# A gated graph kernel: the adjacency product cut into 64x64x64 pieces, and w4's product reordered

## What the reference computes

```python
h = relu(layernorm(x))                       # first layer: attention
q, k, v = h @ Wq.T, h @ Wk.T, h @ Wv.T
rel = adj.T * (q @ k.T); rel = rel / norm(rel, axis=2)
x = x + rel @ v
h = relu(layernorm(x)); h0 = h               # second layer: a gated network, three steps
for _ in range(3):
    a = adj @ h                              # per graph; in and out matrix are the same adj
    z = sigmoid(w3([a, a]) + b3 + u3(h) + bu3)
    r = sigmoid(w4([a, a]) + b4 + u3(h) + bu3)
    hv = tanh(w5([a, a]) + b5 + u5(r * h) + bu5)
    h = (1 - z) * h + z * hv
x = x + h
```

## Time and profile before

| what | us |
|---|---|
| median of three runs | 908.33 |
| the profiled execution, its own time | 907.36 |
| its span on the core | 905.6 |
| PE busy | 891.7 |
| DVE (VectorE) busy | 756.7 |
| ACT (ScalarE) busy | 520.9 |
| POOL busy | 111.0 |

### The profile page before, as it was taken

One profiled execution on the slowest core, in us unless ns is written; L12 is line 12 of the kernel. 1 busy time (PEld: TensorE's weight loads), 2 busy tenths in 40 slices (PEclk: granted clock), 3 DMA queues, 4 the chain that ended last, 5 costly groups with the idle time before them and its releaser, 6 DMA issues.

```text
span 905.6 us, 15070 instructions
## 1 busy us (share of the span) xinstructions
PE 891.7 (98%) x4984; PEld 763.0 (84%) x4984; DVE 756.7 (84%) x1527; ACT 520.9 (58%) x892; POOL 111.0 (12%) x161
## 2 busy tenths in 40 slices
PE   8999999999999999999999999999999999999996
PEld 7878888888888888888888888888888888888885
DVE  6888879888799888988988888988879888798665
ACT  5465664656456564665645656556664656555552
POOL 2110102101021010210101101120101101020000
PEclk9999999999999999999999999999999999999998
DMA  6023222623235142441414513154221622233212
GB/s 182 6 69 114 93 94 99 203 69 113 90 123 184 46 142 89 140 167 42 150 58 141 184 69 116 46 176 148 93 93 70 203 98 93 93 116 117 87 54 93
DMA packets 75394, 98.73 MB, mean 109 GB/s; under 512 B 8176, under 2 KB 65776, under 8 KB 75376
## 3 DMA queue, kind: packets, MB, share of 16 engines
q1 hardware_dynamic: 75376, 98.50, 33.0%
HBM read 50.76 MB, written 47.71 MB: 109 GB/s over the span
## 4 chain that ended last, share of the span: by engine, by line
PE 95%; DVE 2%; issue 1%; DMA 1%; ACT 1%; SPq 0%; DVEq 0%
PE gate L410 14%; PE gate L411 14%; PE gate L412 14%; PE cand L410 10%; PE cand L412 9%; PE cand L411 9%; PE fea L564 9%; PE tok L410 3%; PE tok L411 2%; PE tok L412 2%; PE fea L497 2%; PE fea L411 1%; PE fea L410 1%; PE fea L412 1%; DMA x_s<-x 1%
## 5 line engine op out<-in xcount | busy, mean ns | idle before, releaser
L808 ACT ACTIVATE r_s<-gate,b_r 128x512 f32<-128x512 f32 x96 | 65.7, 690 | 123.8 <-PE gate L412 123.8
L1129 DVE TENSOR_TENSOR rh<-r_s,h 128x512 f32<-128x512 f32 x96 | 69.8, 760 | 29.5 <-ACT r_s L808 28.9
L821 ACT ACTIVATE z_s<-gate,b_z 128x512 f32<-128x512 f32 x96 | 64.1, 683 | 48.0 <-PE gate L412 48.0
L827 ACT ACTIVATE c_s<-cand,b_c 128x512 f32<-128x512 f32 x96 | 64.4, 686 | 26.2 <-PE cand L412 25.5
L724 ACT ACTIVATE h_hi<-h 128x512 fp32r<-128x512 f32 x92 | 56.8, 628 | 38.1 <-DVE h L921 22.4
L355 POOL TENSOR_TENSOR rstd<-vare,minus_half 128x4 f32<-128x4 f32 x32 | 42.0, 1312 | 297.3 <-DVE vare L955 297.3
L410 PE MATMUL gate<-h_hi,W_hi_u 128*128 128x512 f32 x192 | 77.9, 406 | 0.2 <-DVE h_lo L921 0.2
L1101 DVE SCALAR_TENSOR_TENSOR d_s<-z_s,h 128x512 f32<-128x512 f32 x96 | 63.5, 685 | 17.5 <-ACT z_s L821 17.5
L410 PE MATMUL cand<-rh_hi,W_hi_u 128*128 128x512 f32 x192 | 76.5, 398 | 0.0
L410 PE MATMUL gate<-a_hi,W_hi_w 128*128 128x512 f32 x192 | 75.0, 390 | 1.1 <-DVE a_lo L921 1.1
L411 PE MATMUL gate<-h_lo,W_hi_u 128*128 128x512 f32 x192 | 75.1, 391 | 0.0
(11 more groups left out here) (150 smaller groups left out, 2202.7 us busy)
## 6 DMA issues: line engine op xcount, KB each, us to landing
h_back<-h_trip SPq DMA_DIRECT2D x216, 128.0 KB, 2.8
h_trip<-h_turned SPq DMA_DIRECT2D x40, 512.0 KB, 2.6
out<-o_s SPq DMA_DIRECT2D x16, 512.0 KB, 3.8
x_s<-x SPq DMA_DIRECT2D x15, 512.0 KB, 4.9
hx_trip<-hx SPq DMA_DIRECT2D x14, 512.0 KB, 3.5
hx_back<-hx_trip SPq DMA_DIRECT2D x56, 128.0 KB, 2.8
h_trip<-h_blk SPq DMA_DIRECT2D x14, 512.0 KB, 3.0
h_trip_last<-h_turned SPq DMA_DIRECT2D x7, 512.0 KB, 3.5
```

The costliest lines, as they stand in the source:

```text
L808: nc.scalar.activation(r_s[:, c, :], gate[:, c, :], ACT.Sigmoid, bias=b_r[:, c:c + 1]).then_inc(r_ready, 1)
L821: nc.scalar.activation(z_s[:, c, :], gate[:, c, :], ACT.Sigmoid, bias=b_z[:, c:c + 1]).then_inc(z_ready, 1)
L827: nc.scalar.activation(c_s[:, c, :], cand[:, c, :], ACT.Tanh, bias=b_c[:, c:c + 1]).then_inc(c_ready, 1)
L1129: nc.vector.tensor_tensor(rh[:, c, :], r_s[:, c, :], h[s][:, c, :], ALU.mult).then_inc(rh_ready, 1)
```

## The change

Three parts. First, the adjacency product is 32 matmuls of 64x64 by 64x64 in place of eight of 128x128 by 128x128. Each takes 64 nodes (one graph, e) and 64 features (f) as stationary operand and one diagonal block of `adjT` as moving one. Graph e reads partitions of half e and writes into PSUM bank e; feature half f lands in output partitions of half f. So `fea` is now one bank for each graph of a pair, both chunks in it, and the two `split_a` work by bank e, writing a_hi and a_lo in runs of 64 columns. Both banks are released together at the end. A semaphore `sources_seen`, which nobody waits for, is incremented once or twice in each adjacency by TensorE's sequencer, behind the waits. Second, w4's product does all eight matmuls that take a_hi, then waits for a_lo, then does the four that take a_lo; the first output half (o = 0) now ends two matmuls before the second. Third, u3's and w4's product of window 1 move from the head of the loop to its foot, so that TensorE jumps back behind w4's product.

```diff
+        def set_columns(t, e):
+            return t[:].rearrange("p c (q e n) -> p c q e n", q=Q, e=2)[:, :, :, e, :]
+
+        def set_bank(e):
+            return fea[:, e, :].rearrange("p (c q n) -> p c q n", c=C, q=Q)
...
-            def adjacency(c, src, n):
-
-                fea_wait(n, c)
-                for q in range(Q):
-                    last = nc.tensor.matmul(fea[:, c, graph_pair(q)], src[:, q, c * P:(c + 1) * P], adjT[:],
-                                            start=True, stop=True)
-                last.then_inc(fea_full, 1)
+            def adjacency(src, n, t_full=None):
+                fea_wait(n, 1)
+                for c in range(C):
+                    if t_full is not None:
+                        pe.wait_ge(t_ready, t_full + c)
+                    if c == 0 or t_full is not None:
+                        pe.sem_inc(sources_seen, 1)
+                    for q in range(Q):
+                        for f in range(2):
+                            part = slice(c * P + f * N, c * P + (f + 1) * N)
+                            for e in range(2):
+                                last = nc.tensor.matmul(set_bank(e)[half(f), c, q, :], src[half(e), q, part],
+                                                        adjT[half(e), half(e)], start=True, stop=True)
+                last.then_inc(fea_full, 2)
...
             def reset_gate_a(w, s, n_a):
-                for c in range(C):
-                    pe.wait_ge(a_hi_ready, 2 * w + (c + 1))
-                    pe.wait_ge(fea_taken, 2 * n_a + (c + 1))
-                    for o in range(C):
-                        last = product(gate[:, o, :], weight("w4", c, o), (a_hi[s][:, c, :], a_lo[s][:, c, :]),
-                                       False, c == C - 1)
-                        if c == C - 1:
-                            last.then_inc(r_full, 1)
+                pe.wait_ge(a_hi_ready, 2 * w + 2)
+                for o in range(C):
+                    for c in range(C):
+                        w_hi, w_lo = weight("w4", c, o)
+                        one(gate[:, o, :], w_hi, a_hi[s][:, c, :])
+                        one(gate[:, o, :], w_lo, a_hi[s][:, c, :])
+                pe.wait_ge(fea_taken, 2 * n_a + 2)
+                for o in range(C):
+                    for c in range(C):
+                        last = one(gate[:, o, :], weight("w4", c, o)[0], a_lo[s][:, c, :], stop=c == C - 1)
+                    last.then_inc(r_full, 1)
...
+            def first_reset_gate(i):
+                pe.wait_ge(h_lo_new, 4 * i + 4)
+                reset_gate_h(6 * i + 1, 1)
+                reset_gate_a(6 * i + 1, 1, use_in_round("adj 0", i - 1))
...
+            first_reset_gate(0)
             with pe.Fori(0, PAIRS - 1) as i:
                 for k in (1, 2, 3, 4, 5):
                     window(i, k, lambda name: use_in_round(name, i))
                 window(i + 1, 0, lambda name: use_in_round(name, i))
+                first_reset_gate(i + 1)
...
-            def split_a(s, c, n):
-                fea_wait(n, c)
-                copy(a_hi[s][:, c, :], fea[:, c, :]).then_inc(a_hi_ready, 1)
+            def split_a(s, e, n):
+                fea_wait(n, e)
+                copy(set_columns(a_hi[s], e), set_bank(e)).then_inc(a_hi_ready, 1)
...
-                sub(a_lo[s][:, c, :], fea[:, c, :], a_hi[s][:, c, :]).then_inc(fea_taken, 1)
+                sub(set_columns(a_lo[s], e), set_bank(e), set_columns(a_hi[s], e)).then_inc(fea_taken, 1)
```

More of the change, by code:

```diff
@@ L186, in gated_graph_kernel @@
         tok_taken = sem("tok_taken")
+        sources_seen = sem("sources_seen")
         h_is_turned, h_out, h_in, t_ready = sem("h_is_turned"), sem("h_out"), sem("h_in"), sem("t_ready")
@@ L412, in product, with one @@
                 return nc.tensor.matmul(dst, l_lo, r_hi, start=False, stop=stop, skip_group_check=True)
+            def one(dst, lhs, rhs, start=False, stop=False):
+                return nc.tensor.matmul(dst, lhs, rhs, start=start, stop=stop, skip_group_check=True)
             def weight(n, c, o):
@@ L637, in window @@
                     pe.wait_ge(h_lo_new, 4 * i + 2)
-                elif k == 1:
-                    pe.wait_ge(h_lo_new, 4 * i + 4)
-                else:
+                elif k > 1:
                     pe.wait_ge(h_lo_ready, 8 * i + 2 * (k - 1))
-                reset_gate_h(w, s)
-                reset_gate_a(w, s, use("adj %d" % (k - 1)) if k > 1 else use_in_round("adj 0" if k else "adj 5", i - 1))
+                if k != 1:
+                    reset_gate_h(w, s)
+                    reset_gate_a(w, s, use("adj %d" % (k - 1)) if k else use_in_round("adj 5", i - 1))
                 candidate_a(w, s)
@@ L657, in window @@
                         pe.wait_ge(h0_plain, 2 * i + 1)
-                        adjacency(0, h0[o], use("adj 5"))
-                        adjacency(1, h0[o], use("adj 5"))
+                        adjacency(h0[o], use("adj 5"))
                 elif k == 0:
                     pe.wait_ge(h0_plain, 2 * i)
-                    adjacency(0, h0[o], use("adj 0"))
-                    adjacency(1, h0[o], use("adj 0"))
-                else:
-                    for c in range(C):
-                        pe.wait_ge(t_ready, 8 * i + 2 * k + (c - 1))
-                        adjacency(c, t_s, use("adj %d" % k))
+                    adjacency(h0[o], use("adj 0"))
+                else:
+                    adjacency(t_s, use("adj %d" % k), 8 * i + 2 * k - 1)
             pe.wait_ge(const_ready, 1)
@@ L696, in _ @@
             pe.wait_ge(adj_in, 32)
-            adjacency(0, h0[0], n("adj first"))
-            adjacency(1, h0[0], n("adj first"))
+            adjacency(h0[0], n("adj first"))
             reset_gate_h_start()
@@ L708, in _ @@
             candidate_rh(0, 0)
-            adjacency(0, h0[1], n("adj 0"))
-            adjacency(1, h0[1], n("adj 0"))
+            adjacency(h0[1], n("adj 0"))
             tok_done(n("new 0"))
+            first_reset_gate(0)
             with pe.Fori(0, PAIRS - 1) as i:
@@ L1053, in split_state, with split_a @@
                     sub(h_lo[o][:, c, :], h[o][:, c, :], h_hi[o][:, c, :]).then_inc(h_lo_ready, 1)
-            def split_a(v, s, c):
-                dve.wait_ge(a_hi_ready, 2 * v + (c + 1))
-                sub(a_lo[s][:, c, :], fea[:, c, :], a_hi[s][:, c, :]).then_inc(fea_taken, 1)
+            def split_a(v, s, e):
+                dve.wait_ge(a_hi_ready, 2 * v + (e + 1))
+                sub(set_columns(a_lo[s], e), set_bank(e), set_columns(a_hi[s], e)).then_inc(fea_taken, 1)
             def turn_h0(g, s, w):
```

## The result

After the change the kernel takes 918.42 us, the median of four runs (915.40 to 919.44), against 908.33 before: a ratio of 1.010 [1.0085, 1.0115]. It is 1% slower. The forecast was 887 us with a range of 882 to 906, so it was wrong in sign and outside its range.

The account below looks back on a forecast made before the run. TensorE (PE) was taken as the bound, busy 891.7 of 905.6 us. 907.36 - 23.5 (adjacency) + 0.6 + 1.4 (a_lo waits) - 0.3 (first window 1) = 885.6; with 0.97 for the median 886.5, said as 887; range 882 to 906.

Parts of the forecast that it names:

- Part three: the jump: TensorE's loop end: the 208 ns jump stays hidden behind w4's product; gain 0, keeping up to 1.4 us from being lost.
- The cover: At the jump behind w4's product: that product's 2.7 us hides the jump instruction of 208 ns.
- Part one: Adjacency product on TensorE: 1.28 us in place of 1.78, 0.50 saved each, 23.5 us over 47 adjacencies.
- Four in flight: 16 steps: New adjacency's 64 records overlap in fours: 16 steps of 0.056 us, 0.89 plus 0.39 for edges, 1.28 us.
- the rival at 927: Two records in flight: the adjacency costs 2.18 us, 0.40 more than before, 47 times 18.8 us, so 927; chance 0.14.
- the scores' 1.08 / 32: In the two-in-flight rival: PE's possible feeding limit from the scores' 32 records, given as 29 ns; 64 x 0.034 are 2.16.
- Part two: w4's product reordered: a_lo wanted 5.84 us behind the adjacency instead of 4.02, second a_lo ready at 5.55, 0.29 in time.
- 0.3 us in this window: w4's product without the reorder: PE arrives 4.02 us behind the adjacency and waits 0.3 us for a_lo.
- The waits for a_lo: PE waiting for VectorE's second a_lo: 0.6 us over seven rounds in window 1, 1.4 us in windows 5 and 0.
- the prediction's sign: In the profile after, a wait of PE for a_lo of 1 to 3 us in all would show the forecast right.
- Writing in runs of 64 columns: ScalarE's a_hi and VectorE's a_lo keep their size and only write in runs of 64 columns: costed at nothing.
- own range of 882 to 893: Whole kernel: range of the main forecast, with edges 0.1 us smaller or the waits doubled; chance 0.68.

Follow-up runs that it names:

- experiment with q innermost: The changed kernel with TensorE's rounds written out and q as innermost loop, so eight records in a row use one quarter of the array: 953.11 us, one run.
- written-out version: The changed kernel with TensorE's seven rounds written out instead of looped, so its sequencer never jumps: 893.59 us, ratio 0.9827 to the kernel before.
- VectorE's other order: The changed kernel with rounds written out, and both a_lo splits ahead of VectorE's second turn of the state: 888.74 us, ratio 0.9781 to before.

## Why the prediction was wrong

**The step that failed** is the whole of "Part three: the jump", and in it the sentence "Its instruction takes 208 ns and is hidden today ... behind w4's product, 2.7 us, it is. Gain 0". It took the price of the jump from a row of a 1315-instruction body and kept it for one of 1893. The prediction itself counts the records, 16 and then 64 for each adjacency; six windows of 48 more are 576 more instructions, and nothing asked what they cost beyond their matmuls. No rival named it either, and the range, made from what matmuls and VectorE might do, left it out. Measured: 4.1 us for the instruction, 4.1 us of the kernel per taken jump on average (3.1 to 5.6 by the traces, more where the clock falls), 24.8 in all. The section of the Trainium skill cited above names this danger, and it wasn't weighed.

The cover was wrong as well. "2.7 us" is the length of w4's product, but not what is queued when the sequencer gets to the jump. A wait on a semaphore holds the sequencer, and the one for a_lo stands in the middle of that product: VectorE's second a_lo ends at 504.51, the first matmul that takes it starts at 504.56, and the jump at 504.67. PE's timeline at the jump:

```profile
504.18 0.39 PE L422 MATMUL gate<-a_hi,W_lo_w 128*128 128x512 f32 x1
504.56 1.19 PE L422 MATMUL gate<-a_lo,W_hi_w 128*128 128x512 f32 x4
508.88 0.49 PE L417 MATMUL cand<-a_hi,W_hi_w 128*128 128x512 f32 x1 [3.12 <-issue]
```

Four matmuls lie behind the wait, 0.9 us at 0.228. Even so the move is worth 4.8 us here, and parts two and three together 0.26% with the old adjacency.

**Part one: right.** The chain has the adjacency and its first follower at

```profile
498.72 1.09 PE fea L581 x64
499.81 0.43 PE gate L417
```

1.09 + 0.43 - 0.23 = 1.29 against the 1.28 forecast; by whole windows without a late a_lo, 15.40 less 14.92 and 14.95, or 16.85 less 16.33 in windows 3 and 5, the saving is 0.45 to 0.52, some 22.6 us in all and not 23.5. "Four in flight: 16 steps" holds. The timeline cut just behind an adjacency's first record (294.800) and uncut:

```profile
294.77 0.29 PE L581 MATMUL fea<-adjT,t_s 64*64 64x64 f32 x4
```

```profile
294.77 1.16 PE L581 MATMUL fea<-adjT,t_s 64*64 64x64 f32 x64
```

Four records start within 0.03 us, though the program has the two records of each matmul together. The strict order of the Trainium skill, "TensorE: Matmul & The Clock Gate", Part 3, would allow two; the measurement decides against it for these products, and the rival at 927 with it. The experiment with q innermost puts the other end beside it: there the records of one quarter start 0.05 us or more apart, so two records of one quarter don't start together, and the four here are of four quarters. That rival also has a slip: it gives the scores' 1.08 / 32 as 29 ns, where it is 34, the figure that its 2.16 us is made from. Neither limits how fast PE is fed, for 64 records in 1.09 us are 17 ns each.

**Part two: right in kind, low in size for what it prevents.** The prediction gave "0.3 us in this window" as the wait without the reorder. It is 0.94 in the mean of all windows (46.8 us), since with one bank per graph even the first six matmuls need both a_lo. The prediction still took the first a_lo alone there; by its own times for the second, 5.55 against 4.02, the wait would have been 1.5 us.

**The waits for a_lo: too low.** 0.6 us were forecast in window 1 and 1.4 in windows 5 and 0. The written-out version has none in windows 5 and 0 (16.33 and 14.94 us), but some in windows 1, 2 and 4. Window 2 before, in the written-out version, and in the change, where the pause at the jump lets VectorE catch up; then window 1 in the written-out version:

```profile
507.68:529.98 22.30, 22.30 (x146) 19.25 (x144) 18.90 (x38) 11.74 (x22) 1.01 (x1) 1.00 0.22 73
```

```profile
501.64:523.91 22.27, 22.11 (x193) 18.34 (x192) 18.88 (x38) 12.11 (x23) 1.01 (x1) 1.00 0.24 82
```

```profile
518.86:540.68 21.82, 21.82 (x193) 18.41 (x193) 18.64 (x38) 11.58 (x21) 1.01 (x1) 1.00 0.18 59
```

```profile
486.46:501.64 15.18, 15.18 (x125) 12.09 (x124) 13.83 (x30) 9.74 (x19) 2.73 (x3) 1.00 0.53 177
```

Window 2 gains 0.03 us in place of 0.48, window 4 gains 0.11 (22.34 to 22.23), and window 1 gains 0.22. Added up over the rounds, some 8.5 us are lost by late a_lo. PE's list shows only 2.8, and the prediction's sign (1 to 3 us of waits for a_lo) would have passed: the list counts only the time in which no matmul record runs, and a record lasts 0.39 where the step is 0.228. In this step 0.32 us are lost, and 0.16 are listed:

```profile
507.18 0.39 PE L422 MATMUL gate<-a_hi,W_lo_w 128*128 128x512 f32 x1
507.73 0.96 PE L422 MATMUL gate<-a_lo,W_hi_w 128*128 128x512 f32 x3 [0.16 <-DVE a_lo L941]
```

**VectorE and ScalarE.** Writing in runs of 64 columns costs a_hi and a_lo nothing that shows (595 and 669 ns in the mean; 598 and 668 before):

```profile
L744 ACT ACTIVATE a_hi<-fea 128x512 fp32r<-128x512 f32 x96 | 52.1, 595 | 17.6 <-PE fea L581 17.6
```

```profile
L941 DVE TENSOR_TENSOR a_lo<-fea,a_hi 128x512 fp32r<-128x512 f32 x96 | 64.2, 669 | 0.4
```

**The sum again**, from forecast to result:

| step | us |
|---|---|
| forecast | 887 |
| saving by the adjacency 22.6 instead of 23.5 | 0.9 |
| late a_lo, 8.5 by the trace instead of 2 (VectorE's other order gives 4.9 back) | 6.5 |
| not accounted for | -0.8 |
| the change without a jump, measured | 893.6 |
| six taken jumps: 19.7 idle, some 7 from the lower clock (an estimate: 15.5 us of steps at 0.43 in place of 0.228), less the a_lo waits that the pause saves | 24.8 |
| the change, measured | 918.4 |

The forecast's own range of 882 to 893 misses even the version without a jump, by 0.6 us. What stays open: whether the limit is bytes or the number of pieces, and where between 108.7 and 114.9 KB it lies; what decides whether the clock falls behind a pause (1.91 us were enough twice, 3.21 and 3.19 were not); and the price of the `sources_seen` increments by themselves, which was not tried.

## What to carry to other kernels

When a change multiplies instructions inside a loop, count the body of each engine in instructions and bytes before costing anything else: here the jump went from 0.2 to 4.1 us between 1699 and 1796 instructions of PE, and the loop written out, or two of six windows left in the old form, kept all or most of the gain. When a matmul's record is longer than the step, measure whole windows from start to start, not only listed waits. A jump's cover is what is queued behind the last wait ahead of it, not the product that it stands behind. And a wait called "issue", or one for something that was ready long ago, once per round and at one place, is the sequencer; look for the jump and for the packets of code.

## What the runs showed of the hardware

- PE's code: a body of 108.7 KB jumps back in 0.215 us, one of 114.9 KB in 4.29 us, and nine pieces of 16 KB are brought anew in each round. Code written out in full is brought by DMA too (0.95 MB), with no wait of PE that shows it.
- Behind the six jumps of the change, after 3.1 to 3.4 us without work, the granted clock fell to 0.50 four times, for 3.4 us or 6.8 (the fifth), and stayed at 1.00 twice. At the fourth the fall began 1.3 us after work had resumed (510.18 against 508.88), at the fifth, 619.41, while PE still idled.
- 64x64x64 float32 records start in fours, 0.058 us from four to four (294.880, 294.939, 294.997 in the trace), if neighbours go to different quarters; eight in a row on one quarter make it 2.62 us.
